# Decayed operands split out of PSUM, and a lead of 22 tiles of maxima, in a one-core hybrid network kernel

## The reference, cut to what matters

```
q = x @ W_q;  k = x @ W_k;  v = x @ W_v
latent_kv = (k + v) @ W_down_kv
k_rec = (latent_kv @ W_up_k)   # per head: b, 16, s, 8
v_rec = (latent_kv @ W_up_v)
scores = einsum('bhqd,bhkd->bhqk', qh, k_rec) / sqrt(d)
decay = exp(-0.01 * abs(t[:, None] - t[None, :]))
attn = softmax(scores * decay, axis=-1)
out = einsum('bhqk,bhkd->bhqd', attn, v_rec)
```

## Time and profile before

| | before |
|---|---|
| median of 3 executions | 1121.29 us |
| profiled execution: time | 1125.32 us |
| its span, first to last instruction | 1123.5 us |
| mean granted TensorE clock | 0.982 |
| preparation of the attention, first QKV matmul to last value matmul | 241.3 to 269.8 us |
| lead, first to last unit on DVE | 278.2 to 309.0 us |
| steps with units | 309.0 to 633.9 us |
| steps without units | 633.9 to 678.7 us |

### The profile page before, as it was taken

One profiled execution on the slowest core, in us unless ns is written; L12 is line 12 of the kernel. 1 busy time (PEld: TensorE's weight loads), 2 busy tenths in 40 slices (PEclk: granted clock), 3 DMA queues, 4 the chain that ended last, 5 costly groups with the idle time before them and its releaser, 6 DMA issues.

```text
span 1123.5 us, 15969 instructions
## 1 busy us (share of the span) xinstructions
PE 1041.1 (93%) x6036; PEld 413.5 (37%) x6048; DVE 743.8 (66%) x1194; ACT 678.7 (60%) x1140; POOL 170.5 (15%) x119
## 2 busy tenths in 40 slices
PE   5799998988999999999999989999989988999998
PEld 2233333335433333333333334443333333334443
DVE  2787326348989999999999621126879898881110
ACT  4687525446078788888888774467556656634331
POOL 0222531006000000000000000000333342340000
PEclk9899999999989999999999999999989999999999
DMA  8000000038950321303000000000000000000000
GB/s 270 1 2 1 1 0 1 0 123 233 303 90 4 64 43 23 65 4 63 9 3 8 7 2 1 1 1 0 1 0 1 0 1 0 1 10 1 10 9 10
DMA packets 31203, 38.37 MB, mean 34 GB/s; under 512 B 7964, under 2 KB 22300, under 8 KB 30744
## 3 DMA queue, kind: packets, MB, share of 16 engines
q1 hardware_dynamic: 31128, 37.37, 13.2%
HBM read 23.23 MB, written 13.86 MB: 33 GB/s over the span
## 4 chain that ended last, share of the span: by engine, by line
PE 51%; DVE 23%; ACT 6%; issue 2%; another core or an unknown queue 1%; DVEq 0%; ACTq 0%
PE PS L1510 17%; DVE ffn L926 15%; PE PS L1038 6%; PE PS L1014 4%; DVE PS L1063 2%; PE PS L1495 2%; PE PS L1498 2%; PE PS L1521 2%; ACT arena L1048 2%; PE PS L1577 1%; PE PS L1080 1%; PE PS L1687 1%; PE PS L916 1%; DVE arena L1724 1%; PE PS L1677 1%
## 5 line engine op out<-in xcount | busy, mean ns | idle before, releaser
L1048 ACT ACTIVATE arena<-PS 128x384 f32<-128x384 f32 (+1 forms) x512 | 258.0, 547 | 84.4 <-PE PS L1014 72.9
L926 DVE CUSTOM_DVE_ANT_0 ffn<-PS,XP 128x1024 bf16<-128x1024 f32 x256 | 300.7, 1216 | 4.4 <-PE PS L916 4.4
L916 PE MATMUL PS<-arena 48*128 48x512 bf16 (+3 forms) x704 | 173.6, 325 | 5.6 <-DVE MX L926 5.5
L1014 PE MATMUL PS<-arena 50*128 50x512 bf16 (+3 forms) x640 | 169.4, 320 | 1.6 <-ACT arena L1048 1.3
L1038 PE MATMUL PS<-arena 128*32 128x256 f32 x2048 | 162.4, 393 | 1.0
L1540 ACT ACTIVATE arena<-PS,w_scl 128x512 f32<-128x512 f32 x64 | 43.5, 687 | 139.5 <-PE PS L1510 139.2
L1510 PE MATMUL PS<-arena,w_h2T 128*128 128x512 f32 x256 | 118.0, 607 | 0.0
L1510 PE MATMUL PS<-arena,w_h1T 128*128 128x512 f32 x256 | 115.3, 594 | 0.4 <-DVE arena L1549 0.4
L1014 PEld LDWEIGHTS PS<-arena 50*128 50x128 bf16 x640 | 50.4, 94 | 101.9 <-ACT arena L1048 70.2
L1724 DVE TENSOR_TENSOR_SCAN arena<-arena 128x512 f32<-128x512 f32 x64 | 81.4, 1273 | 0.3
L1510 PEld LDWEIGHTS PS<-arena,w_h2T 128*128 128x128 f32 x256 | 49.6, 195 | 61.1 <-issue 58.6
(11 more groups left out here) (228 smaller groups left out, 1558.0 us busy)
## 6 DMA issues: line engine op xcount, KB each, us to landing
arena<-scr SPq DMA_DIRECT2D x64, 192.0 KB, 5.7
scr<-arena SPq DMA_DIRECT2D x16, 384.0 KB, 5.5
scr<-arena SPq DMA_DIRECT2D x16, 256.0 KB, 4.9
scr<-arena SPq DMA_DIRECT2D x16, 128.0 KB, 3.3
XP<-xT SPq DMA_DIRECT2D x1, 1024.0 KB, 4.9
w_h1T<-h1T SPq DMA_DIRECT2D x1, 1024.0 KB, 6.7
w_h2T<-h2T SPq DMA_DIRECT2D x1, 1024.0 KB, 8.6
arena<-MH SPq DMA_DIRECT2D x64, 4.0 KB, 1.7
```

Of the source, the lines that this page charges most:

```text
L916: mm = t.matmul(PS[:, bank, k0 - lo:k1 - lo], packed(m, g, v, slice(q * P, (q + 1) * P), KP), packed(m, g, 2 + v, slice(k0, k1), KP), star ...
L926: v.tensor_tensor_reduce(JUNK[:, u % 2, :], PS[:, bank:bank + 2, :].rearrange("p a b -> p (a b)"), STRIP[:, at:at + S], 1.0, -3.0e38, ALU. ...
L1014: mm = t.matmul(PS[:, score_bank(T, i), at:at + b_ - a_], packed(n, g, 2 + v, slice(kt * P, (kt + 1) * P), KP + MROWS), packed(n, g, v, sl ...
L1048: nc.scalar.activation(PT[:, T % 2, score_head(T, i), a0_:a1_], PS[:, score_bank(T, i), a0_:a1_], ACT.Exp).then_inc(s_free, 1)
```

## The change

The change does five things.

1. DVE writes the four decayed operands into PSUM banks 5, 0, 6 and 3 (`DECAYED`) and not into `V32`. ACT rounds them from there, and the rest is read from PSUM and written to `V32`. The wait on `a1_lo_free` moves from the decayed operands to the rests. The value copy now stands between rests 1 and 2.
2. Bank 0 is also the output of the q projection, and bank 3 that of the reconstructed keys. So PE waits for rests: the QKV matmuls of chunk c for the first two rests of chunk c-1 (before: for the first two decayed operands), and the key matmul for all four. Ahead of the lead PE waits for all 16.
3. `LEAD` goes from 26 to 22. The turns move from steps 8j-5 to 8j-3, `RING` from 116 to 118, and the projections, `LN5_AT` and `SIXTH_FREE` move with it.
4. The maxima of a turn are written by two DMAs (32 rows each) and not by four (16 rows each), so `pk_m` counts by 32.
5. On SP `maxima(0)` and its wait for the even chunks' stores stand ahead of `packs(1)`, and the wait for the odd ones behind it.

```diff
--- before.py
+++ after.py
@@ -737,7 +737,7 @@
         STORES = 16 * 4 * 3
         NSTEP, NUNIT = NGRP * NS, NGRP * NT1
         NTH, KH = NT1 // 2, NKT // 2
-        LEAD = NTH + 10
+        LEAD = NTH + 6
         S_BANKS, D_BANK, O_BANK = (0, 1, 4, 5), 2, 3
         RING = (NUNIT - LEAD) // 2 + 1
         HEADS = (0, 2, 1, 3)
@@ -760,6 +760,8 @@
         def is_diag(T):
             return T % 2 == 0
 
+
+        DECAYED = (5, 0, 6, 3)
 
         def a1_prep_pe(t):
             wait_loads(t, 3)
@@ -767,7 +769,7 @@
                 x = XN[:, c * CH:(c + 1) * CH]
                 t.wait_ge(ln_free, ln_count(4, c))
                 if c > 0:
-                    t.wait_ge(a1_ver, 4 * c - 2)
+                    t.wait_ge(a1_r1, 4 * c - 2)
                 t.matmul(PS[:, 0, :], wqkv1[:, 0:P], x, start=True, stop=True)
                 t.matmul(PS[:, 1, :], wqkv1[:, P:2 * P], x, start=True, stop=False)
                 t.matmul(PS[:, 1, :], wqkv1[:, 2 * P:3 * P], x, start=False, stop=True).then_inc(a1_qkv, 1)
@@ -778,6 +780,8 @@
                 t.wait_ge(a1_latc, c + 1)
                 t.wait_ge(ln_free, ln_count(4, NCH - 1))
                 t.wait_ge(a1_v, c + 1)
+                if c > 0:
+                    t.wait_ge(a1_r1, 4 * c)
                 t.matmul(PS[:, 3, :], wlow[:, P:2 * P], LAT, start=True, stop=True)
                 for w in range(CH // P):
                     mm = t.matmul(PS[:, 4, w * P:(w + 1) * P], LAT[:, w * P:(w + 1) * P], wlow[:, 2 * P:3 * P],
@@ -802,7 +806,7 @@
                     a.wait_ge(a1_stored[c % 2], STORES)
                 for v in range(4):
                     a.wait_ge(a1_ver, 4 * c + v + 1)
-                    nc.scalar.copy(SPL[c % 2][:, v, 0, :], V32[c % 2][:, v, :]).then_inc(a1_hi, 1)
+                    nc.scalar.copy(SPL[c % 2][:, v, 0, :], PS[:, DECAYED[v], :]).then_inc(a1_hi, 1)
                 if c + 1 < NCH:
                     take_kv(c + 1)
                     take_latent(c + 1)
@@ -822,16 +826,21 @@
                     c = b * 2 + j
                     v.wait_ge(a1_qkv, c + 1)
                     for n, tab in ((0, FALL), (1, RISE), (2, RISE), (3, FALL)):
-                        v.wait_ge(a1_lo_free, 4 * c + n + 1)
                         if n == 2:
                             v.wait_ge(a1_kr, c + 1)
-                        v.scalar_tensor_tensor(out=V32[j][:, n, :], in0=PS[:, 0 if n < 2 else 3, :],
+                        v.scalar_tensor_tensor(out=PS[:, DECAYED[n], :], in0=PS[:, 0 if n < 2 else 3, :],
                                                scalar=SCALE if n < 2 else 1.0, in1=tab[:, j * CH:(j + 1) * CH],
                                                op0=ALU.mult, op1=ALU.mult).then_inc(a1_ver, 1)
+
+                    def rest(n):
+                        v.wait_ge(a1_hi, 4 * c + n + 1)
+                        v.wait_ge(a1_lo_free, 4 * c + n + 1)
+                        v.tensor_tensor(V32[j][:, n, :], PS[:, DECAYED[n], :], SPL[j][:, n, 0, :], ALU.subtract).then_inc(a1_r1, 1)
+                    rest(0)
+                    rest(1)
                     v.tensor_copy(XN[:, chunk(c)], PS[:, 4, :]).then_inc(a1_v, 1)
-                    for n in range(4):
-                        v.wait_ge(a1_hi, 4 * c + n + 1)
-                        v.tensor_tensor(V32[j][:, n, :], V32[j][:, n, :], SPL[j][:, n, 0, :], ALU.subtract).then_inc(a1_r1, 1)
+                    rest(2)
+                    rest(3)
 
         def a1_minus_ones(g):
 
@@ -943,7 +952,7 @@
 
         def maxima_dve(v, j):
             if j >= 2:
-                v.wait_ge(pk_m, 64 * (j - 1))
+                v.wait_ge(pk_m, 32 * (j - 1))
             v.wait_ge(m_t, j + 1)
             rows = slice(0, 2 * NTH)
             v.tensor_copy(MH[rows, j % 2, 0, :], PS[rows, D_BANK, 0:P]).then_inc(m_h, 1)
@@ -1106,9 +1115,9 @@
 
         TURNS = {maxima_at(j): j for j in range(1, 2 * NGRP)}
         PROJ_FROM = (NUNIT - LEAD) // 2 + 1
-        PROJ_PE = {PROJ_FROM: ((0, 0), (0, 1)), PROJ_FROM + 1: ((0, 2), (0, 3)), PROJ_FROM + 2: ((1, 0), (1, 1)),
-                   PROJ_FROM + 3: ((1, 2), (1, 3)), NSTEP - 4: ((2, 0), (2, 1)), NSTEP - 3: ((2, 2),), NSTEP - 1: ((2, 3),)}
-        LAST_SUMS, LN5_AT, SIXTH_FREE = NSTEP - 4, NSTEP - 9, NSTEP - 4
+        PROJ_PE = {PROJ_FROM: ((0, 0), (0, 1), (0, 2)), PROJ_FROM + 1: ((0, 3), (1, 0), (1, 1)), PROJ_FROM + 2: ((1, 2), (1, 3)),
+                   NSTEP - 3: ((2, 0), (2, 1)), NSTEP - 2: ((2, 2),), NSTEP - 1: ((2, 3),)}
+        LAST_SUMS, LN5_AT, SIXTH_FREE = NSTEP - 4, NSTEP - 8, NSTEP - 3
         RECIPROCAL_AT = 6
 
         def idle_pe(t, times, bank):
@@ -1120,6 +1129,7 @@
             a1_prep_pe(t)
             idle_pe(t, 18, 7)
             t.wait_ge(a1_v, 1 + NCH)
+            t.wait_ge(a1_r1, 4 * NCH)
             for u in range(LEAD):
                 unit_pe(t, u, 0)
                 unit_pe(t, u, 1)
@@ -1144,7 +1154,7 @@
                     elif T + 1 < NSTEP:
                         diag_pe(t, T + 1, heads)
                 if s % NKT == 0:
-                    t.wait_ge(pk_m, 64 * (T // NKT + 1))
+                    t.wait_ge(pk_m, 32 * (T // NKT + 1))
                 if s == 0:
                     t.wait_ge(vg_in, n + 1)
                 after_turn = T - 1 in TURNS
@@ -1292,11 +1302,10 @@
             def maxima(j):
                 sp.wait_ge(m_l, j + 1)
                 n, hf = divmod(j, 2)
-                for half in range(2):
-                    for k in range(2):
-                        row = 64 * half + KP + k
-                        dst = PK[row:row + 1, n % NSLOT, 0, hf, :, :].rearrange("p a (t q) -> p (a t) q", q=P)
-                        sp.dma_start(dst, MH[NTH * half:NTH * half + NTH, j % 2, k, :]).then_inc(pk_m, 16)
+                for k in range(2):
+                    dst = PK[KP + k:KP + k + 65:64, n % NSLOT, 0, hf, :, :].rearrange("p a (t q) -> p (a t) q", q=P)
+                    src = MH[0:2 * NTH, j % 2, k, :]
+                    sp.dma_start(dst, src).then_inc(pk_m, 16)
 
             def denominators(n):
                 sp.wait_ge(o_free, 2 * n + 2)
@@ -1325,10 +1334,10 @@
             packs(0)
             stores(2)
             stores(3)
+            sp.wait_ge(a1_stored[0], 2 * STORES)
+            maxima(0)
             packs(1)
-            sp.wait_ge(a1_stored[0], 2 * STORES)
             sp.wait_ge(a1_stored[1], 2 * STORES)
-            maxima(0)
             packs(2)
             maxima(1)
             packs(3)
```

## The result

The changed kernel took 1129.13 us (median of 17 executions, 1127.6 to 1137.26) and the kernel before 1124.81 us in the same sessions (17 executions, 1120.0 to 1128.14). The ratio is 1.0053, with an interval of 1.0035 to 1.007. That is 6.0 us slower (3.9 to 7.9), where 9.5 us were forecast. The median itself lies only 1.7 us from the forecast 1130.8 us; part of that is luck, since the kernel before also came out 3.5 us longer here than in the three executions that the forecast started from. The profiled execution of the changed kernel took 1133.61 us.

What follows compares the result with a forecast made beforehand. It took PE's serial chain to bound the preparation, DVE the lead and loop, PE the tail, with ACT close. 8.7 + 5.4 - 4.6 + 5.2 - 5.2 = +9.5 us gave 1130.8 us, range 1124.0 to 1136.0.

Steps and rivals of the forecast that it cites:

- Part 1, the wait: Preparation: PE's QKV matmuls wait for rests 1 and 2, 2.9 us for each of three chunks, +8.7 us.
- the cover assumed for the others: Preparation: QKV groups and idle matmuls hide the other new waits, otherwise 1.8 us a chunk and 4.4 us once.
- Part 1, the clock: Preparation: a low-clock stretch behind each of three new PE gaps, +5.4 us, between 0 and 8.7.
- POOL blocks no rest: Preparation: rests with one operand in PSUM are not held up beside POOL, taken as 0.
- The old row's 2.0 us: Rival, chance 0.06: in the preparation POOL still blocks rests, 1.0 us in each of two chunks, 1132.8 us in all.
- Parts 2 to 4: Four units fewer in the lead, -4.6 us; two more loop steps with units, +5.2; shorter tail, -5.2.
- the tail: Steps without units: -3.0 us up to step 121, -2.1 after it, some 0.6 against; -5.2, between -4.5 and -6.9.
- half output of step 120: Tail: it now stands behind two squares on ACT, costing some 0.6 us.
- Part 5, transfers: Maxima and packed-group transfers around the lead's end and early loop: nothing waits, 0 us.
- that rival (+2.4 to +4.1): Rival, chance 0.17: the clock holds in the preparation, so about 1124.5 us.
- wait for maxima: Rival, chance 0.08: in the loop maxima land late behind a packed group, 3.7 us a wait, 1134 to 1142 us.
- the waits on PE were not short: Rival, chance 0.07, claimed short preparation waits, under 1.5 us a chunk, making the kernel faster; 1118.2 us at 0.5.

Runs made afterwards that it cites:

- idle matmuls in the wait: The changed kernel with ten idle matmuls on PE ahead of the QKV wait of chunks 1 to 3, the wait kept; ratio 1.0054 to before, median 1128.08 us.
- bank 7: The changed kernel with the second decayed query in free PSUM bank 7, so PE's QKV matmuls wait as before; ratio 0.9961 to before, 1118.86 us.
- lead only: The changed kernel with the operands, rests and waits of before, keeping the new lead, tail and transfers; ratio 0.9959 to before, 4.6 us faster.

## Why the prediction was right in sign, and where its size was off

**Part 1, the wait: right.** Forecast +8.7 us; the preparation with the clock held is 8.5 us longer, and three chunks without a low stretch at 9.97 us would make 8.7. The three QKV groups wait 2.67 us each for a rest, and the cover assumed for the others was there: no row of after shows PE waiting at the key matmul or ahead of the lead for a rest.

**Part 1, the clock: right in kind, mis-sized.** This is the step that was off: "So I expect a low stretch behind each of three new gaps". The profiled execution did just that and lost 6.0 us: its three QKV groups took 4.5, 5.5 and 4.5 us instead of the 2.9 us of before. But over four profiles the clock fell at 6 gaps of 12, and 1.6 us for a preparation with one low stretch is what three of them show. So the price of a stretch was nearly right (1.8 us forecast, 1.4 to 2.0 measured); their number was not. The executions without a profile agree. From each one's mean clock and span the time at low clock is 2 x (1 - clock) x span. On average it is 36.4 us before (29 executions) and 40.7 and 41.1 us in the two sessions of the changed kernel (17 and 9): 4.3 to 4.7 us more, some 1.3 low stretches, not three. With idle matmuls in the wait it is 36.8 us (12). These are means over whole executions, so they hold the other stages too. Within one kernel's executions, each microsecond at low clock goes with about 0.35 us of time. So the term is some 1.5 us by the executions (4.3 x 0.35), up to 2.4 us by the profiles (1.5 stretches at 1.6), not 5.4.

Seven gaps of seven in the earlier trace rows were all of one execution, and a count from one execution says little of how often. The profile of after already answers it: the gap of 1.68 us at 886.6 of before, which had a low stretch behind it, stands there too, without one. Before, and then after:

```profile
888.25 0.39 PE L1671 MATMUL PS<-arena,trib 128*128 128x512 bf16 x1 [1.68 <-DVE arena L1715]
888.20:892.00 3.80, 3.54 (x11) 0.90 (x12) 3.80 (x5) 2.58 (x4) 2.04 (x2) 0.61 0.00 0
```

```profile
898.09 0.39 PE L1680 MATMUL PS<-arena,trib 128*128 128x512 bf16 x1 [1.67 <-DVE arena L1724]
898.20:902.00 3.80, 3.59 (x15) 1.13 (x15) 3.80 (x5) 2.44 (x3) 1.88 (x2) 1.00 0.01 2
```

This gap stands in all eleven profiles of this case, and the clock fell behind it in two. The Trainium skill (TensorE: Matmul & The Clock Gate, section "Part 1: The HAM clock gate") says that how many matmuls run slow at a kernel's start varies from run to run. The runs here show such a variation in mid-kernel, 3 gaps of 3 in one profile of the changed kernel and 1 of 3 in the other. The forecast should have given each stretch a chance.

With 1.6 us in the place of 5.4 the sum is 8.5 + 1.6 - 4.6 + 5.5 - 5.6 = +5.4 us, and 6.0 (3.9 to 7.9) were measured.

**POOL blocks no rest: right.** All 16 rests took 677 to 680 ns, also those beside POOL (the two from 262.28 on, while POOL worked from 260.68 to 264.06), where one took 1.68 us before.

```profile
L838 DVE TENSOR_TENSOR SQ<-PS,arena x8: 677/678/680, 250.6 to 277.3; 128x512 f32<-128x512 f32 x8
L838 DVE TENSOR_TENSOR arena<-PS,arena x8: 677/678/680, 262.3 to 289.0; 128x512 f32<-128x512 f32 x8
```

The old row's 2.0 us were the wrong end of the bound. The Trainium skill (SBUF — State Buffer, section "SBUF: two separate sides") has a DVE instruction take the ports that it shares with GpSimd if it has two SBUF inputs. These rests have one, and the trace agrees. The delays that this removes were hidden: bank 7, which has the short rests too, can't be told from lead only.

**Parts 2 to 4: right in sum, the tail by two errors that cancel.** Lead -4.6 (30.8 to 26.2), loop +5.5 for +5.2, tail -5.6 for -5.2. Lead only measured their sum: -4.6 us. In the tail the stretch up to the start of step 121 takes 15.8 us (650.31 to 666.10), where the sum of its parts gave 14.8: -2.0 us and not -3.0. That sum left out waits of PE, such as one of 0.58 us for ACT, which the 17.8 us of before contained and which came again. The seven steps behind it take 23.4 us: -3.7 and not -2.1. The reason for this is the low stretch at 664, which did not come in this profile (clock 1.00 from 664 to 668); the prediction's own figure without it was -3.9. Other profiles have one that begins at 662 to 673. The half output of step 120 does stand behind the two squares on ACT.

**Part 5, transfers: right for this kernel, and for the reason that the lead was late.** With the wait removed, the same edits are worth 3.4 us (order) and up to 3.3 us (number). The prediction costed them at nothing. It gave a reason for the packed groups, but did not ask what the old order and the four DMAs cost once the lead is early: 4.0 to 5.0 us of waiting at step 0.

**The rivals.** The clock does not hold in every execution, nor is it lost in every one; the truth lies between that rival (+2.4 to +4.1) and the forecast (+9.5). No wait for maxima appeared in the loop of after, and the waits on PE were not short (2.67 us each).

**Two readings.** Both are off and change no term. The first unit in the earlier trace rows follows the idle matmuls with no gap, not after 0.07 us. And PE's gap at 914.2 in the earlier trace rows is 1.43 us long by its timeline, not at most 1.2.

**What stays open:** why the clock falls at the second gap in all four profiles and behind the others in one (at the second it falls 0.5 to 0.7 us before PE begins again, while PE still stands), and what brings the low stretch early in the loop. Also open is what makes the longest executions: the kernel with idle matmuls has them too, 3 of 12 at 1132.8 to 1134.2 us, so the gaps of the preparation alone don't explain them.

## What to carry to other kernels

When an operand moves to PSUM, ask which engine wrote that bank and when it needs it next: here one bank shared with the next chunk's first matmul cost 8.5 us, and a free bank cost nothing that could be measured. Count a clock loss behind a short gap as a chance, from several executions, not as a certainty from one. And test an edit that seems to be worth nothing again once the stall that covers it is gone.

## What was not expected of the hardware

Gaps of 2.67 us on PE, alike in length and in the work around them, had a low stretch in 6 of 12 cases. Ten idle matmuls in each brought it to 0 of 3. Two small DMAs issued behind eight loads on the same queue held PE for 4.0 us, and issued ahead of them for none. The 17 executions of the changed kernel spread with their mean clock: nine took 1127.6 to 1129.1 us at 0.985, three 1136.6 to 1137.3 us at 0.974, and five lie between.
